# One attention block and one expert on one core: the same steps in another order, with about fifty of them on another engine

## The chip, the cores and the metric

The kernel runs on one core of one Trainium2 chip. The metric is the device time of one launch in microseconds. A profiled execution also gives a span, the time from the first to the last instruction of the core.

## The reference, cut to what matters

x has 2 batches of 2048 rows of 128 values. Two stages follow, each a layer norm, a network, a layer norm of its result and a sum.

```python
def attn(h, Wq, Wk, fc1_w, fc1_b, fc2_w, fc2_b):          # 1 head of 128
    q, k = rope(bf16(h @ Wq.T)), rope(bf16(h @ Wk.T))
    scores = (q @ k.T) / 128 ** 0.5
    o = where(causal, exp(scores), 0.0).sum(axis=-1)       # only the row sums are used
    return relu(o @ fc1_w.T + fc1_b) @ fc2_w.T + fc2_b     # 1 -> 16 -> 128

def ffn(x, W1, b1, W2, b2):                                # one of 16 experts has all the weight
    return relu(x @ W1[1] + b1[1]) @ W2[1] + b2[1]         # 128 -> 256 -> 128

x = x + layernorm(attn(layernorm(x)))
x = x + layernorm(ffn(layernorm(x)))
```

## The kernel before, in words

**Tiles.** The 4096 rows are 8 groups of 4 tiles of 128 rows; groups 0 to 3 are batch 0, groups 4 to 7 batch 1. Each stage has a list of the pieces it works on. FRONTS (norm, transpose, q, k and rope) are numbered 0 to 8: group 0 in two halves (0 and 1), then groups 1, 4, 5, 2, 6, 3, 7 as 2 to 8. BACKS (scores to the hidden layer) are groups 0, 1, 4, 5, 2, 6, 3 as 0 to 6, and the two halves of group 7 as 7 and 8. OUTS (the second product, last norm, sum and store) are the same as BACKS to 6 and then the four single tiles of group 7 as 7 to 10. Because of the causal mask a group needs the keys of the groups before it in its batch.

**Steps.** The whole program is the table STEPS, one word for each step, as `name.number`. A letter behind it gives the engine where there is a choice (A for ACT, D for DVE, P for POOL, which is GpSimd), and `#` gives the PSUM banks, of which there are eight. Each engine walks through the same table and issues, in that order, the steps that are its own. It waits on a semaphore for what a step reads, and where a bank was used before, until the user before has been emptied (Banks.free). So the table fixes the order on every engine, and an engine that waits holds up everything behind it in its own queue.

The steps of one piece are, in order:

- load_x (SP, DMA of x), stat1 (DVE, BN_STATS over pairs of tiles, L631), eps1 (variance plus epsilon, L354 on DVE and POOL, L602 on ACT), rstd1 (POOL, power of minus one half, L489), norm1 (x times rstd, L348);
- tr1 (PE, 4 transposes, L716), +tr1 (the copy out of PSUM, L505), q and k (PE, float32 matmuls, L724), +q and +k (copies to bfloat16, L505);
- the rotated half for rope either by swap (SP, two DMAs that exchange the partition halves, L336 and L337) or by rot (PE, L734); cos, sin (products with a table, L380 on POOL in two halves, L383 on DVE, L407 from PSUM) and rope (the sum, L414 to L417);
- scores.n.j.s (PE, L750 and the mask's L754) for row tile j and the key segment s: segment 0 is the keys of the first two groups of the batch, segment 1 those of the third and fourth, so that a group 2 or 3 of a batch can do its segment 1 before the first two are ready; exp (ACT, L553, in place, with the row sum); sum (DVE, L362 or L364), hT (PE, L761), +hT (ACT, relu, L522), fc2 (PE, L777 or L769);
- stat3, eps3, rstd3, x1 (the first stage's result, L664); stat4, eps4, rstd4, norm4, trz (PE, L716), +trz, h0 and h1 (PE, L724), +h0 and +h1 (relu with bias, ACT L528, DVE L530);
- y (PE, 8 matmuls of 128 columns for a group, L798, in some pieces on top of the bias by a matmul of ones, L788; in others bias on DVE, L679), stat5 (DVE L638 or ACT L609), eps5, rstd5, out (DVE L664, or ys on DVE, L650, and the sum on POOL, L496), store (SP, L341).

blank is a matmul on zeros whose result is not used (L693); blank.8 are eight of 512 columns. wqk and w1 centre the weights on PE, w2mean, b2mean and the like prepare the others on ACT. SP issues every DMA, in the order of the table. In the profile each float32 matmul stands as two instructions.

Of the kernel before, what the change touches and what calls it, by code (L numbers as in the profile page):

```python
# [35 lines left out]


STEPS = """
load_x.4 blank.8#7 blank.1.256#7 load_x.3 mask.0 load_wqk.0 load_x.1 load_x.0 repeat.0 stat1.4 load_fc.0 eps1.4.D
stat1.3 rstd1.4 load_x.6 wqk.0#0 load_x.8 eps1.3.A stat1.1 rstd1.3 eps1.1.A norm1.4.D load_x.5 blank.1#7 blank.1.256#7  # L40
+wqk.0.A load_x.2 stat1.0 tr1.4#1 rstd1.1 norm1.3.D load_b2.0 fc.0#0 +tr1.4.A load_table.1 norm1.1.P stat1.6 tr1.3#2
fcmean.0 load_table.0 q.4#1 eps1.0.D +tr1.3.A eps1.6.P stat1.8 load_x.7 rstd1.6 tr1.1#3 load_table.3 +q.4.A k.3#2
stat1.5 load_w2.0 +fc.0 rstd1.0 norm1.6.D q.3#1 load_table.2 eps1.8.D norm1.0.D tr1.6#4 +k.3.D rstd1.8 +q.3.A k.4#0
eps1.5.D +tr1.1.A stat1.2 swap.3 +tr1.6.A norm1.8.P tr1.0#3 stat1.7 +k.4.A q.1#1 load_table.4 k.6#4 cos.3.D w2mean.0
load_b1.0 eps1.2.D q.6#0 +tr1.0.D rstd1.2 +k.6.A swap.4 cos.4.D w2.0 q.0#3 sin.3.D +q.6.A tr1.8#4 load_w1.0 rstd1.5
k.0#2 b2mean.0 rope.3.D swap.6 +q.0.A k.1#0 +q.1.A norm1.2.D scores.2.3.0#3 +tr1.8.A scores.2.1.0#1 cos.6.D
scores.2.0.0#5 exp.2.3.0 scores.2.2.0#6 tr1.2#7 sin.4.D +k.1.A q.8#4 exp.2.1.0 cos.1.D exp.2.2.0 rope.4.D k.8#0 +k.0.A
+tr1.2.A eps1.7.D +q.8.D norm1.5.P scores.3.0.0#12 exp.2.0.0 +k.8.D scores.3.1.0#67 exp.3.0.0 rstd1.7 rot.1#5 sum.2.D
scores.3.3.0#34 swap.8 cos.8.D exp.3.1.0 hT.2#0 rot.0#1 sin.1.D cos.0.P k.2#2 exp.3.3.0 sin.0.D scores.3.2.0#56
rope.1.D +k.2.A q.2#7 rope.0.D +hT.2 sin.6.D exp.3.2.0 scores.0.1.0#2 scores.0.2.0#0 tr1.5#3 sin.8.D w1.0#4 +q.2.A  # L50
sum.3.D rope.8.D fc2.2#56 exp.0.1.0 swap.2 +tr1.5.A cos.2.D hT.3#7 scores.7.1.0#12 +w1.0.A rope.6.D scores.0.3.0#3
+hT.3 q.5#4 exp.7.1.0 stat3.2.D norm1.7.P k.5#7 +q.5.D exp.0.2.0 exp.0.3.0 eps3.2.D scores.5.3.0#12 sin.2.D exp.5.3.0
+k.5.D rstd3.2 scores.8.3.1#34 rope.2.D swap.5 exp.8.3.1 x1.2 cos.5.P scores.1.3.0#12 fc2.3#07 exp.1.3.0 stat4.2
scores.1.0.0#56 scores.0.0.0#3 tr1.7#4 stat3.3.D exp.1.0.0 scores.1.2.0#12 +tr1.7.D exp.0.0.0 eps3.3.P scores.1.1.0#56
exp.1.2.0 rstd3.3 sum.0.D sin.5.D q.7#4 exp.1.1.0 eps4.2.P x1.3 hT.0#1 scores.5.1.0#23 rstd4.2 +hT.0 scores.8.2.1#56
exp.5.1.0 rope.5.D fc2.0#01 +q.7.D norm4.2.P scores.4.2.1#7 exp.8.2.1 scores.4.1.1#2 stat3.0.D scores.4.0.1#3 k.7#4
exp.4.2.1 stat4.3 eps3.0.P scores.4.1.0#56 exp.4.0.1 rstd3.0 sum.1.D exp.4.1.1 +k.7.D trz.2#7 exp.4.1.0
scores.7.0.0#23 eps4.3.D +trz.2.D swap.7 rstd4.3 x1.0 exp.7.0.0 scores.5.0.0#45 norm4.3.P hT.1#6 h1.2#7 exp.5.0.0
stat4.0 scores.8.2.0#23 eps4.0.D +h1.2.D scores.4.2.0#01 +hT.1 rstd4.0 exp.8.2.0 scores.4.3.0#45 cos.7.D trz.3#7
sin.7.D h0.2#6 exp.4.3.0 +trz.3.D norm4.0.P scores.4.0.0#23 +h0.2.D exp.4.2.0 scores.4.3.1#7 trz.0#4 rope.7.D fc2.1#56  # L60
exp.4.3.1 +trz.0.D scores.6.0.0#01 exp.4.0.0 stat3.1.D h0.0#4 eps3.1.D exp.6.0.0 rstd3.1 scores.6.3.0#23 +h0.0.D
h0.3#7 exp.6.3.0 sum.4.D x1.1 hT.4#4 scores.6.2.1#01 +hT.4 scores.6.2.0#23 exp.6.2.1 stat4.1 scores.6.0.1#45 h1.0#6
+h0.3.D exp.6.0.1 fc2.4#01 exp.6.2.0 +h1.0.D scores.6.1.0#45 eps4.1.D stat3.4.D scores.6.3.1#67 rstd4.1 exp.6.1.0
y.2#2 eps3.4.D rstd3.4 norm4.1.D b2.0 exp.6.3.1 b2split.0 x1.4 scores.5.0.1#4 scores.5.2.1#5 exp.5.0.1 scores.5.1.1#3
scores.5.2.0#67 exp.5.2.1 bias.2.D scores.5.3.1#4 exp.5.1.1 scores.6.1.1#01 exp.5.2.0 trz.1#5 stat5.2.D h1.3#3
+trz.1.D eps5.2.P exp.6.1.1 rstd5.2 stat4.4 scores.8.3.0#67 y.0#5 exp.5.3.1 b2rows.0 eps4.4.P exp.8.3.0 rstd4.4
sum.5.D sum.6.D +h1.3.D hT.5#4 norm4.4.P scores.7.0.1#67 ys.2 +hT.5 scores.7.1.1#01 exp.7.0.1 bias.0.D hT.6#3 h0.1#4
out.2.P +hT.6 stat5.0.D exp.7.1.1 fc2.5#67 eps5.0.P store.2 h1.1#3 stat3.5.D sum.7.D fc2.6#01 +h0.1.D eps3.5.P +h1.1.A
rstd3.5 trz.4#2 stat3.6.A hT.7#3 y.1#4 rstd5.0 x1.5 eps3.6.A +trz.4.A rstd3.6 sum.8.D +hT.7 ys.0 h1.4#2 stat4.5
out.0.P h0.4#5 bias.1.D eps4.5.A +h1.4.A x1.6 fc2.7#3 rstd4.5 store.0 +h0.4.A hT.8#2 y.3#6 stat5.1.A stat4.6 norm4.5.P  # L70
stat3.7.D eps3.7.A eps4.6.D +hT.8 rstd4.6 trz.5#0 bias.3.D y.4#1 +trz.5.A stat5.3.D rstd3.7 norm4.6.D eps5.3.A x1.7
rstd5.3 fc2.8#0 trz.6#3 stat3.8.A out.3 h0.5#2 +trz.6.A eps3.8.A stat4.7 h1.5#5 store.3 rstd3.8 stat5.4.D eps4.7.A
+h0.5.A h0.6#6 rstd4.7 eps5.1.D x1.8 +h1.5.A rstd5.1 eps5.4.D h1.6#2 stat4.8 +h0.6.D y.5#5 rstd5.4 +h1.6.A norm4.7.D
eps4.8.D rstd4.8 ys.4 norm4.8.D trz.7#1 out.1 out.4.P stat5.5.A y.6#2 +trz.7.D eps5.5.A store.4 rstd5.5 store.1
trz.8#1 stat5.6.D h0.7#4 +trz.8.A h1.7#6 +h0.7.A eps5.6.P h0.8#1 +h1.7.D rstd5.6 h1.8#0 out.5 +h0.8.A y.7#6 +h1.8.A
y.8#1 stat5.7.A out.6 store.5 y.10#5 eps5.7.P stat5.8.A rstd5.7 y.9#0 stat5.10.A eps5.8.D store.6 out.7 rstd5.8
stat5.9.A eps5.10.D store.7 rstd5.10 eps5.9.A out.8 store.8 rstd5.9 out.10 store.10 out.9 store.9
# [761 lines left out]
```

## Time and profile before

| | |
|---|---|
| runs, us | 92.93, 95.62, 94.38 (median 94.38) |
| the profiled execution | 92.96 us |
| its span | 91.2 us |
| PE busy | 82.5 us (90%), 445 matmul instructions |
| DVE busy | 78.5 us (86%) |
| ACT busy | 70.7 us (78%) |
| POOL busy | 59.2 us (65%) |
| mean granted clock of TensorE | 0.992 |

The busy shares are over the whole span; PE's include time in which one matmul's end overlaps the next one's start. PE is the matmul part of TensorE, PEld its weight loads, DVE is VectorE, ACT is ScalarE, POOL is GpSimd and SP issues DMAs.

### The profile page before, as it was taken

The numbers are of one execution on the slowest core, as the hardware profiler recorded it, in microseconds if no ns is written. First come the engines' busy times: TensorE is split into PE (matmuls) and PEld (weight loads), VectorE is DVE, ScalarE is ACT, GpSimd is POOL, SyncE is SP. The second block draws the span as 40 slices with busy tenths as digits, with TensorE's granted clock in tenths as the row PEclk, the third lists the DMA queues.
The fourth block names the chain that finished last, engine by engine and source line by source line (L and its number), as shares of the span: only waits on it lengthen the run. The fifth ranks groups of instructions, "written<-read, shape, count | busy, mean of one in ns | idle before, by whom it ended". The sixth has DMA issues, their size and how long they took to land.

```text
span 91.2 us, 1530 instructions
## 1 busy us (share of the span) xinstructions
PE 82.5 (90%) x445; PEld 49.4 (54%) x445; DVE 78.5 (86%) x205; ACT 70.7 (78%) x201; POOL 59.2 (65%) x84
## 2 busy tenths in 40 slices
...
DMA packets 11884, 7.64 MB, mean 84 GB/s; under 512 B 851, under 2 KB 10980, under 8 KB 11876
## 3 DMA queue, kind: packets, MB, share of 16 engines
...
## 4 chain that ended last, share of the span: by engine, by line
PE 59%; ACT 14%; DVE 9%; DMA 7%; issue 3%; SPq 2%; POOL 2%; POOLq 1%; DVEq 0%
PE psum L724 19%; PE psum L798 14%; ACT psum L553 11%; PE psum L750 11%; PE psum L716 6%; DMA x_s<-x 4%; PE psum L777 3%; DMA qk_swap<-qk 3%; DVE rows_n L348 2%; POOL rstd L489 2%; ACT fc L566 2%; DVE qk_r L383 2%; DVE qk_swap L383 2%; PE psum L769 1%; DVE qk L505 1%
## 5 line engine op out<-in xcount | busy, mean ns | idle before, releaser
L489 POOL TENSOR_TENSOR rstd<-ve,half_neg 128x4 f32<-128x4 f32 (+2 forms) x38 | 35.0, 930 | 23.1 <-DVE ve L354 18.7
L553 ACT ACTIVATE psum<-psum 128x1024 f32<-128x1024 f32 (+7 forms) x48 | 36.6, 763 | 1.2 <-PE psum L754 0.8
L750 PE MATMUL psum<-qk_r 128*128 128x512 bf16 (+3 forms) x80 | 19.7, 348 | 1.7 <-DVE qk_r L417 1.0
L798 PE MATMUL psum<-w_c,hid 128*128 128x128 f32 x128 | 16.0, 277 | 0.0
L798 PEld LDWEIGHTS psum<-w_c,hid 128*128 128x128 f32 x128 | 15.5, 192 | 0.8 <-issue 0.3
L724 PE MATMUL psum<-cols_n,wqk 128*128 128x512 f32 (+1 forms) x36 | 15.8, 553 | 0.0
L724 PE MATMUL psum<-cols_n,w_c 128*128 128x512 f32 (+1 forms) x36 | 15.7, 550 | 0.0
L750 PEld LDWEIGHTS psum<-qk_r 128*128 128x128 bf16 x80 | 6.7, 98 | 13.0 <-ACT psum L553 4.8
L716 PE MATMUL psum<-ident,rows_n 128*128 128x128 f32 x64 | 10.2, 277 | 0.9 <-DVE rows_n L348 0.9
L638 DVE BATCH_NORM_STATS2 stats<-psum 128x6 f32<-128x256 f32 x23 | 8.7, 419 | 1.5 <-PE psum L798 1.0
L664 DVE SCALAR_TENSOR_TENSOR x<-psum,rstd,x_s 128x128 f32<-128x128 f32 x32 | 9.1, 343 | 1.0 <-POOL rstd L489 0.9
L716 PEld LDWEIGHTS psum<-ident,rows_n 128*128 128x128 f32 x64 | 7.3, 141 | 4.6 <-issue 2.1
L553 ACT ACTIVATION_READ_ACCUMULATOR psum<-psum 128x1 f32 x48 | 9.1, 189 | 0.0
L631 DVE BATCH_NORM_STATS2 stats<-x_s 128x6 f32<-128x256 f32 x16 | 6.2, 423 | 2.7 <-DMA x_s<-x 2.4
L505 ACT ACTIVATE cols_n<-psum 128x512 f32<-128x512 f32 (+1 forms) x11 | 6.0, 558 | 2.7 <-PE psum L716 2.7
L724 PEld LDWEIGHTS psum<-cols_n,w_c 128*128 128x128 f32 x36 | 6.1, 190 | 2.8 <-issue 2.0
L724 PEld LDWEIGHTS psum<-cols_n,wqk 128*128 128x128 f32 x36 | 6.1, 190 | 2.8 <-issue 1.4
L528 ACT ACTIVATE hid<-psum,b_s 128x512 f32<-128x512 f32 (+1 forms) x9 | 5.5, 615 | 2.7 <-PE psum L724 2.6
L609 ACT ACTIVATE rows_n<-psum 128x128 f32<-128x128 f32 x18 | 4.8, 278 | 3.2 <-PE psum L798 1.9
L602 ACT ACTIVATE ve<-stats,small 128x4 f32<-128x4 f32 (+2 forms) x10 | 3.0, 296 | 5.5 <-DVE stats L631 4.8
L530 DVE TENSOR_SCALAR hid<-psum,b_s 128x512 f32<-128x512 f32 (+1 forms) x9 | 6.4, 716 | 0.9 <-PE psum L724 0.7
L664 DVE SCALAR_TENSOR_TENSOR x_s<-psum,rstd,x 128x128 f32<-128x128 f32 x20 | 5.8, 345 | 1.1 <-POOL rstd L489 0.8
...
## 6 DMA issues: line engine op xcount, KB each, us to landing
...
```

What stands on the lines that cost most here:

```text
L489: ready[k].done(eng.tensor_tensor(rstd[:, g, STAT_SLOT[k], t], ve[:, g, STAT_SLOT[k], t], half_neg[:, 0:tiles], ALU.pow), n)
L505: return eng.activation(dst, src, ACT.Copy) if on_act else eng.tensor_copy(dst, src)
L528: ins = eng.activation(hid[:, g, h, c], src[:, 0:w], ACT.Relu, bias=b1_s[:, h:h + 1])
L530: ins = eng.tensor_scalar(hid[:, g, h, c], src[:, 0:w], b1_s[:, h:h + 1], 0.0, ALU.add, ALU.max)
L553: exps.done(eng.activation(area, area, ACT.Exp, scale=scale_qk, accum_out=sums[:, g, s, j:j + 1]), n, j, s)
L631: ins = eng.bn_stats(pair_stats(g, k, j), source[:, g, j:j + 2, :].rearrange("p t c -> p c t"))
L638: ins = eng.bn_stats(pair_stats(g, k, j0 + j), net_pair(k, n, j))
L664: ins = eng.scalar_tensor_tensor(dst[:, g, j0 + j, :], area, rstd[:, g, STAT_SLOT[k], j0 + j:j0 + j + 1], prev[:, g, j0 + j, :], ALU.mult, ...
L716: mm = eng.transpose(bank[:, j * P:(j + 1) * P], rows_n[:, g, j0 + j, :], ident[:, :])
L724: made[name].done(eng.matmul(bank_of(name, n)[:, 0:tiles * P], weight, cols_n[:, g, c], start=True, stop=True), n)
L750: mm = eng.matmul(psum[:, own[0] + i, 0:width], query, qk_r[:, g0 + c, 1, 0:width], start=True, stop=c < gb)
L798: mm = eng.matmul(bank[:, j * P:(j + 1) * P], hid[:, g, h, (j0 + j) * P:(j0 + j + 1) * P], w2_c[:, h, :], start=not seeded and h == 0, sto ...
```

## The change

Only the table of steps is another one. It holds the same 496 steps; the fillers blank.1.256 (twice) become blank.1.384 and blank.1.128. Its first words before and after:

```diff
-load_x.4 blank.8#7 blank.1.256#7 load_x.3 mask.0 load_wqk.0 load_x.1 load_x.0 repeat.0 stat1.4 load_fc.0 eps1.4.D
...
+load_x.1 blank.8#7 blank.1.384#7 load_x.3 mask.0 load_wqk.0 load_x.0 load_x.6 stat1.1 repeat.0 load_fc.0 eps1.1.A
...
```

What moves to another engine:

- to DVE: cos.5, norm1.1, norm1.8, norm4.0, norm4.5 (from POOL); +tr1.2, +tr1.4, +k.2, +h0.7, +w1, +wqk, stat3.6, stat5.1, stat5.5 (from ACT);
- to POOL: norm1.0, norm4.1, rope.8, sin.2 (from DVE);
- to ACT: +tr1.0, +k.3, +k.8, +q.8, +trz.1, +trz.7, +h0.0, +h0.6, stat5.0, stat5.3, stat5.4 (from DVE);
- of the 38 small eps steps, 20 change among the three.

The first load is x's piece 1 (128 KB) instead of piece 4 (256 KB). The line numbers of the changed file are one higher than those of the profile.

On DVE the first instructions now are the statistics of pieces 1 and 3, norm1.1, the statistics of piece 0, the weights' copy +wqk and norm1.3; then come the pairs of statistics of pieces 6, 4, 8 and 5 with norm1.6 among them, up to the rows below.

**DVE, the stretch around the first rope.** The names are stats (stat1), rows_n (norm1), ve (eps1), cols_n (+tr1), qk_r (cos, or rope where it reads itself) and qk_swap (sin). Before:

```order
L383 TENSOR_TENSOR qk_r<-qk,table 128x1024
L354 TENSOR_SCALAR ve<-stats 128x4
L505 COPY cols_n<-psum 128x256
L383 TENSOR_TENSOR qk_r<-qk,table 128x1024
L383 TENSOR_TENSOR qk_swap<-qk_swap,table 128x1024
L417 TENSOR_TENSOR qk_r<-qk_r,qk_swap 128x1024
L348 TENSOR_TENSOR rows_n<-x_s,rstd 128x512
L383 TENSOR_TENSOR qk_r<-qk,table 128x1024
```

Now:

```order
L349 TENSOR_TENSOR rows_n<-x_s,rstd 128x512
L632 BN_STATS stats<-x_s 128x6 x2
L384 TENSOR_TENSOR qk_r<-qk,table 128x1024
L349 TENSOR_TENSOR rows_n<-x_s,rstd 128x512
L506 COPY cols_n<-psum 128x512
L632 BN_STATS stats<-x_s 128x6 x2
L384 TENSOR_TENSOR qk_swap<-qk_swap,table 128x1024
L418 TENSOR_TENSOR qk_r<-qk_r,qk_swap 128x1024
L349 TENSOR_TENSOR rows_n<-x_s,rstd 128x512
```

The first rope is L417 before and L418 now, and norm1.2 stands behind it in both. Before, cos.4 and a copy of 256 columns stood ahead of the first sin; now it is norm1.4, norm1.8, two pairs of statistics and a copy of 512 columns, and cos.4 has gone behind.

**POOL, the first half.** rows_n is norm1 or norm4 (norm4 where it reads x1), qk_r is cos or rope, qk_swap is sin. Before:

```order
L489 TENSOR_TENSOR rstd<-ve,half_neg 128x4 x2
L348 TENSOR_TENSOR rows_n<-x_s,rstd 128x512
L489 TENSOR_TENSOR rstd<-ve,half_neg 128x4
L380 TENSOR_TENSOR qk_r<-qk,table 128x256 x2
L348 TENSOR_TENSOR rows_n<-x_s,rstd 128x512
L489 TENSOR_TENSOR rstd<-ve,half_neg 128x4
L380 TENSOR_TENSOR qk_r<-qk,table 128x512 x2
L354 TENSOR_SCALAR ve<-stats 128x4
L489 TENSOR_TENSOR rstd<-ve,half_neg 128x4
L354 TENSOR_SCALAR ve<-stats 128x4
L489 TENSOR_TENSOR rstd<-ve,half_neg 128x4
```

Now:

```order
L355 TENSOR_SCALAR ve<-stats 128x4
L490 TENSOR_TENSOR rstd<-ve,half_neg 128x4
L349 TENSOR_TENSOR rows_n<-x_s,rstd 128x512
L490 TENSOR_TENSOR rstd<-ve,half_neg 128x4 x2
L349 TENSOR_TENSOR rows_n<-x_s,rstd 128x512
L381 TENSOR_TENSOR qk_r<-qk,table 128x256 x2
L381 TENSOR_TENSOR qk_swap<-qk_swap,table 128x512 x2
L355 TENSOR_SCALAR ve<-stats 128x4
L490 TENSOR_TENSOR rstd<-ve,half_neg 128x4
L416 TENSOR_TENSOR qk_r<-qk_r,qk_swap 128x512 x2
L490 TENSOR_TENSOR rstd<-ve,half_neg 128x4 x2
```

Two halves of sin.2 and two of rope.8 have come, and the two halves of cos.5 have gone; rstd and eps of the first stage's results stand behind them.

**PE, around the last scores.** 128x512 x2 at L750 is one score step over two banks. Before:

```order
L750 MATMUL psum<-qk_r 128x512
L750 MATMUL psum<-qk_r 128x256
L754 MATMUL psum<-later,ident_b 128x128
L761 MATMUL psum<-ident,osum 128x128
L724 MATMUL psum<-cols_n,w1_c 128x512
L777 MATMUL psum<-fc2,h1T 128x256 x2
L724 MATMUL psum<-cols_n,w1_c 128x512
L777 MATMUL psum<-fc2,h1T 128x256 x2
L716 MATMUL psum<-ident,rows_n 128x128 x4
L761 MATMUL psum<-ident,osum 64x128
L798 MATMUL psum<-w2_c,hid 128x128 x8
```

Now:

```order
L751 MATMUL psum<-qk_r 128x256
L755 MATMUL psum<-later,ident_b 128x128
L799 MATMUL psum<-w2_c,hid 128x128 x8
L751 MATMUL psum<-qk_r 128x512 x2
L762 MATMUL psum<-ident,osum 128x128
L799 MATMUL psum<-w2_c,hid 128x128 x8
L717 MATMUL psum<-ident,rows_n 128x128 x8
L778 MATMUL psum<-fc2,h1T 128x256 x2
L725 MATMUL psum<-cols_n,w1_c 128x512
L762 MATMUL psum<-ident,osum 64x128
L725 MATMUL psum<-cols_n,w1_c 128x512 x3
L770 MATMUL psum<-fc2,h1T 128x256
```

Before, the last scores (512 and 256 columns and the mask's L754) are followed by hT, h0, fc2, h1, fc2; now one y (L799, eight of them) stands ahead of the last scores (512 columns twice, scores.8.3.0) and one behind, then two trz, and one fc2 of 512 columns and one of 256 (L770) are left behind them.

## Rows read from the trace of the kernel before

**Rows 1.** The page's chain that ended last, shares of the span by engine.

```profile
PE 59%; ACT 14%; DVE 9%; DMA 7%; issue 3%; SPq 2%; POOL 2%; POOLq 1%; DVEq 0%
```

**Rows 2.** Windows of the whole core; busy us of each engine, granted clock.

```profile
core 0: us, PE busy (x) PEld busy (x) DVE busy (x) ACT busy (x) POOL busy (x), PEclk, DMA share, GB/s
17.00:24.00 7.00, 6.24 (x31) 2.94 (x30) 7.00 (x12) 6.09 (x19) 4.15 (x5) 1.00 0.38 95
42.00:52.00 10.00, 10.00 (x47) 4.65 (x45) 9.48 (x24) 10.00 (x23) 4.30 (x4) 1.00 0.08 19
64.00:76.00 12.00, 12.00 (x79) 8.95 (x78) 10.06 (x30) 7.97 (x32) 9.23 (x10) 1.00 0.16 46
```

**Rows 3.** Timeline of PE, head: start, us, engine, line, operation, tiles, [idle before].

```profile
5.64 0.67 PE L699 MATMUL psum<-wqk_f,center 128*128 128x256 f32 x2 [0.88 <-DMA wqk_f<-wqk_t]
...
17.15 0.38 PE L750 MATMUL psum<-qk_r 128*128 128x512 bf16 x1
```

**Rows 4.** Timeline of DVE, head.

```profile
3.50 0.76 DVE L631 BATCH_NORM_STATS2 stats<-x_s 128x6 f32<-128x256 f32 x2 [1.63 <-DMA x_s<-x]
...
5.92 0.43 DVE L631 BATCH_NORM_STATS2 stats<-x_s 128x6 f32<-128x256 f32 x1 [0.80 <-DMA x_s<-x]
...
15.52 0.69 DVE L383 TENSOR_TENSOR qk_swap<-qk_swap,table 128x1024 bf16<-128x1024 bf16 x1 [0.24 <-DMA qk_swap<-qk]
...
16.92 1.53 DVE L348 TENSOR_TENSOR rows_n<-x_s,rstd 128x512 f32<-128x512 f32 x1
...
22.40 1.17 DVE L383 TENSOR_TENSOR qk_r<-qk,table 128x1024 bf16<-128x1024 bf16 x1
```

**Rows 5.** Timeline of ACT: first exponential, a full one, its four waits, the last.

```profile
17.62 0.58 ACT L553 ACTIVATE psum<-psum 128x512 f32<-128x512 f32 x1
...
21.26 0.69 ACT L553 ACTIVATE psum<-psum 128x640 f32<-128x640 f32 x1 [0.76 <-PE psum L754]
...
22.77 1.01 ACT L553 ACTIVATE psum<-psum 128x1024 f32<-128x1024 f32 x1
...
27.94 0.46 ACT L522 ACTIVATE h1T<-psum,fc 128x128 f32<-128x128 f32 x1 [0.40 <-PE psum L761]
...
30.85 1.01 ACT L553 ACTIVATE psum<-psum 128x1024 f32<-128x1024 f32 x1 [0.27 <-PE psum L750]
...
61.15 0.46 ACT L522 ACTIVATE h1T<-psum,fc 128x128 f32<-128x128 f32 x1 [0.37 <-PE psum L761]
...
62.56 0.80 ACT L553 ACTIVATE psum<-psum 128x768 f32<-128x768 f32 x1
```

**Rows 6.** Timeline of PE, from the last scores to the last tile of y.

```profile
61.66 0.28 PE L761 MATMUL psum<-ident,osum 128*128 128x128 f32 x1
...
62.73 0.70 PE L777 MATMUL psum<-fc,h1T 64*128 64x256 f32 x4
...
71.80 0.60 PE L716 MATMUL psum<-ident,rows_n 128*128 128x128 f32 x4
...
86.78 0.66 PE L798 MATMUL psum<-w_c,hid 128*128 128x128 f32 x4
```

**Rows 7.** Timeline of POOL (GpSimd), head.

```profile
12.26 1.04 POOL L348 TENSOR_TENSOR rows_n<-x_s,rstd 128x512 f32<-128x512 f32 x1
14.29 1.98 POOL L489 TENSOR_TENSOR rstd<-ve,half_neg 128x4 f32<-128x4 f32 x2 [0.99 <-DVE ve L354]
16.36 1.55 POOL L348 TENSOR_TENSOR rows_n<-x_s,rstd 128x512 f32<-128x512 f32 x1
...
21.73 1.30 POOL L380 TENSOR_TENSOR qk_r<-qk,table 128x256 bf16<-128x256 bf16 x2
```

**Rows 8.** Groups by line and form, ACT's copies of q and k.

```profile
L505 ACT ACTIVATE qk<-psum 128x512 bf16<-128x512 f32 x7 | 4.2, 595 | 0.5 <-PE psum L724 0.3
```

**Rows 9.** The page's group of the score matmuls: busy us, mean ns, idle before.

```profile
L750 PE MATMUL psum<-qk_r 128*128 128x512 bf16 (+3 forms) x80 | 19.7, 348 | 1.7 <-DVE qk_r L417 1.0
```

**Rows 10.** Chain that ended last, in order of time: the first swap's second half.

```profile
13.01 2.49 DMA qk_swap<-qk
```

More of the change, by code:

```diff
@@ L44 @@
[L44 to L73, printed above, removed]
```

49 lines of the change are left out of this document (40 added, 9 removed).

## Prediction

> **What bounds the kernel now.** I read the page first: of the span of 91.2 us the chain that ended last lies 59% on PE and 14% on ACT [rows 1]. That is a mean over stages, so the windows come next [rows 2]. From 17 to 24 us it is DVE that is full (7.00 of 7.00) while PE and ACT have gaps; from 42 to 52 ACT and PE are both full; from 64 to 76 PE is full (12.00 of 12.00) and ACT is not (7.97). So there are three limits in a row: the head, bound by the loads and DVE; the stretch of the exponentials, bound by ACT with PE close behind; and the end, bound by PE. The granted clock is 1.00 of its upper level in all of them.
>
> The head is read in the timelines of PE and DVE [rows 3, 4]. The first tile group's statistics start at 3.50 us, when x_s has landed; the matmul on Wq and Wk waits for its DMA until 5.64; the first scores start at 17.15. ACT [rows 5] starts its first exponential at 17.62 and ends its last at 62.56 + 0.80 = 63.36: 45.74 us, of which 1.80 are waits (0.76, 0.40, 0.27 and 0.37, in brackets there). From 61.66, when the last scores are through, PE runs to its last tile of y at 86.78 with nothing to wait for [rows 6], and 4.42 us of span lie behind that start.
>
> **The change part by part.** The same operations are done in both: 48 exponentials, the same matmuls and transposes, the same DMAs and bytes. Only the order, the banks and the engine of about 50 steps change. The two fillers of blank columns trade 512 columns for 512 others; they stand in time in which PE waits for loads, and cost nothing while it does. I take the three limits in turn.
>
> *Head.* The first load is now one of 128 KB, then 256, then the weights: these end 512 KB down the queue, and x.0 ends 640 KB down it. Before, 256 KB had landed at 3.50 and 768 KB at 5.92 [rows 4], that is 212 KB/us. So the weights come at 3.50 + 256/212 = 4.7 instead of 5.64, and x.0 at 5.3. PE then has tr1.1 and, after the copy of the weights on DVE, its first q at about 6.2. From there DVE's own queue decides when the first scores can start, because rope.3 stands 18 steps behind x.0's statistics on it. From x.0's landing: its statistics 0.4, the weights' copy 0.35, four norms at 0.60 (a product's 0.69 less the overlap with the next), six pairs of statistics at 0.76, three eps at 0.1, and cos.3, the copy of tr1.4, sin.3 and rope.3 at 0.60 each [rows 4]. That is 0.4 + 0.35 + 2.4 + 4.6 + 0.3 + 2.4 = 10.4, so rope.3 ends at 15.7; with 0.3 for the wait for rstd1.3 and for landings, 16.0. The same three pairs of q and k and the two short ones are in front of the first scores on PE in both orders. Scores start at 16.0 instead of 17.15, and since a transpose stands between the first two, the first exponential starts 1.0 behind: 17.0 instead of 17.62.
>
> Against it stands what DVE and GpSimd do to each other. The norm of 16.92 took 1.53 us instead of about 0.69. It began inside GpSimd's product of 16.36, which ended at 17.91, and ended itself 0.54 later; the product of 22.40 took 1.17 and ended 0.54 behind GpSimd's two halves, at 23.03 [rows 4, 7]. So a DVE product of two operands in SBUF stood still until GpSimd's was done. The Trainium skill (SBUF — State Buffer, Who interferes with whom) says this as a rule: such an instruction and one of GpSimd that reads SBUF take a shared pair of ports in turn, and whoever starts first keeps it for the whole instruction. The trace agrees for products. It does not for rstd: the product that ran from 15.52 to 16.21 took no more than 0.69 beside the two powers of 14.29 to 16.27 [rows 7], so I count no clash with a power. In the changed order norm1.5 on GpSimd (1.04) comes by my count at 12.3 to 13.3, just where norm1.8 stands on DVE. If it starts first, DVE loses up to 0.9 and the first scores start at 16.9, the first exponential at 17.9, 0.3 later than before. The clash may also not occur. I take the middle: first exponential at 17.4, 0.2 earlier.
>
> *Exponentials.* ACT's other work between first and last exponential changes from two short copies, four long ones and the W1 copy (2 x 0.38 + 4 x 0.60 + 0.39 = 3.6) to four long copies, b2mean 0.5, +h0.0 0.69 and an eps of 0.30 (3.9), the long ones by [rows 8]: +0.3. The wait of 0.76 was for scores that wait for rope.4; now scores.5.2.1 and 5.3.1 (group 6 against its own keys alone) stand ahead and fill it. I keep the other 1.0 us of waits, as nothing here says that they go. ACT thus ends exp.6.1.1, the last but one, at 63.36 - 0.2 + 0.3 - 0.76 less the last one's 1.01 [rows 5] = 61.7.
>
> *End.* scores.8.3.0 takes the banks that exp.6.1.1 frees, so PE stands there until then: 61.7 + 0.5 = 62.2 for hT.6 behind it, against 61.66. Behind it PE has less than before: fc2 of two groups (0.63 each, its 0.70 less the overlap) and an hT (0.1) are gone to the front, and one trz (0.44) has come; one y left and one came. That is 0.93 less than 86.78 - 61.66 = 25.12, so 24.19. The last y starts at 62.2 + 24.2 = 86.4 instead of 86.78. The 4.42 behind it stay: the four single tiles, their rstd on GpSimd and the four stores stand in the same order. Sum: 0.4 us by this path with half a clash, 0.8 without it.
>
> The cover of this sum is ACT's 1.0 us of waits. Each that the new order also fills counts in full, since PE's own path (first scores at 16.0, then at most the 69.6 us from 17.15 to 86.78, in which the scores alone waited 1.7 [rows 9]) would reach the last y at about 84. The bounds are therefore: all waits gone and no clash, first exponential 17.0: 86.4 - 0.4 - 1.0 = 85.0, a gain of 1.8; a full clash and 0.76 not won: 86.4 + 0.5 + 0.76 = 87.7, a loss of 0.9. Between ends so far apart I take -0.6, nearer to the sum than to either. The profiled execution took 92.96 us, so the forecast is 92.4. Those 92.96 stand at the lowest of the three runs shown (92.93; median 94.38, highest 95.62), so a median of runs may lie up to 1.4 above such a figure; the range has that inside. 2% is 1.9 us, about what a measurement of this kernel can tell from no change.
>
> **The rivals.** First, *the fill works fully*: no clash in the head, ACT without waits between 17.0 and 61, DVE in front of PE at the end. For it: DVE has about 1 us less in all (products moved to GpSimd, copies to ACT), and ACT's queue has more exponentials that need only one group. Against it: PE and ACT are full in 42 to 52 already. The gain is 1.8 to 2.5, 90.8 us.
>
> Second, *the gain is taken back*: ACT gets about 2 us of work more in all (copies and squares), the clash occurs and other DVE products meet one of GpSimd's six half products of cos, sin and rope, where it had four (1.30 for two of 256 columns [rows 7], so about 1.25 for one of 512). What is won in the head is waited for in the middle: 92.9, between 92.6 and 93.9.
>
> Third, and slower: *rope.8 on GpSimd starves ACT*. Group 7's rope comes at the end of a new chain through both engines. +k.2 ends on DVE 12 instructions behind rope.3, at 16.0 + 6 = 22; its swap lands 3.1 later (0.5 for the first issue, 2.5 and 0.1 behind the second [rows 10]), at 25.1; then sin.2 on GpSimd 2.5, eps and rstd 1.2, x1.2 on DVE 1.1, cos.8 0.6, rope.8 on GpSimd 2.5, with some 0.3 of passing on: 33.3, and 34.2 with the clash. ACT needs scores.7.0.0 after 22 exponentials of 13,440 columns in all (0.84 ns a column and 0.15 us each, from the 0.58 of 512 and the 1.01 of 1024 columns [rows 5]: 14.6) and 3.1 of copies, at 17.0 + 17.7 = 34.7. The slack is 0.5 to 1.4. As soon as two more clashes of 0.9 fall on DVE's or GpSimd's part of it, ACT and PE stand, and everything behind x1.2 with them. At three clashes and the queues behind them the price is 2 to 3: 92.96 + 2.2 = 95.2.
>
> The Trainium skill's rule (SBUF — State Buffer, Who interferes with whom) would, if it held for the powers too, put rstd1.8 and rstd1.5 in DVE's way as well and lead to this third case, 95.2; the product beside the powers in [rows 7] speaks against that, and its chance is inside the 0.15.
>
> **How the numbers follow.** The forecast, a gain of 0 to 1.5, gets 0.42; the full fill 0.24; the gain taken back 0.19; the starved ACT 0.15. The likeliest time is 92.4, its own range 91.4 to 93.0. For 8 in 10 the range reaches from 90.8, the first rival, to 95.0, the third, with the run-to-run spread inside. Faster by over 2% needs 91.1 or less: the full fill and a little of the forecast, 0.25. Slower by over 2%: the third rival and a little of the second, 0.16. Within 2%: 0.59.
>
> **What would show it.** Right: wqk's matmul before 5.0, the first scores between 15.9 and 17.0, no ACT wait of 0.7 near 21, DVE without idle time until 24, the wait of PE at scores.8.3.0 put down to ACT, the last y 24.2 us behind it. A DVE norm of some 1.5 us near 12.5 shows the clash. Wrong: PE's last scores well before ACT is done with them (then PE, not ACT, was the limit), a wait of PE for GpSimd's rope.8 before scores.7.0.0, or ACT waiting for DVE's results in the middle.

## The result and the profile after

| | before | changed |
|---|---|---|
| first comparison, median of its runs | 95.0 us (4 runs, 92.93 to 95.95) | 93.97 us (4 runs, 93.87 to 94.15) |
| first comparison, ratio | | 1.0105 [1.0063, 1.0147] |
| second comparison, median of its runs | 93.86 us (29 runs) | 93.62 us (12 runs) |
| second comparison, ratio | | 1.0031 [0.9987, 1.0076] |
| profiled execution | 92.96 us, span 91.2 | 94.05 us, span 92.2 |

Over all runs of the study 45 of the 97 executions that begin with the order of the kernel before lie over 1.5% above the fastest of their kernel, against 3 of the 100 that begin with the changed order, and the ratios leave all these out (of the first comparison's four of the kernel before only 92.93 remains), which is why they and the plain medians point in opposite directions. By the ratios the change makes the kernel 1.0% slower in the first comparison and 0.3% in the second, whose interval has 1 in it; in the mean that is about 0.6 us. I had forecast 92.4 us, 0.6 us faster.

The page's chain, which answers to [rows 1], has gone over from PE and DVE to ACT (14% before):

```profile
PE 53%; ACT 34%; POOL 4%; DVE 4%; issue 1%; POOLq 1%; DVEq 0%
```

The windows that answer to [rows 2]:

```profile
core 0: us, PE busy (x) PEld busy (x) DVE busy (x) ACT busy (x) POOL busy (x), PEclk, DMA share, GB/s
17.00:24.00 7.00, 7.00 (x36) 3.74 (x34) 6.21 (x13) 7.00 (x24) 2.42 (x2) 1.00 0.59 142
...
32.00:42.00 10.00, 9.18 (x50) 4.32 (x48) 9.87 (x28) 10.00 (x27) 6.73 (x7) 1.00 0.18 40
42.00:52.00 10.00, 9.28 (x45) 4.33 (x45) 9.27 (x27) 10.00 (x24) 5.69 (x6) 1.00 0.01 2
```

From 17 to 24 us DVE is no longer full (6.21 instead of 7.00); PE and ACT are, both with 7.00. The fill that I had expected took place. But ACT is full from there on and PE is not.

The timeline of PE, against [rows 3] and [rows 6]: the centring of Wq and Wk, the first q, the first scores, its waits in the middle, the last scores and the last tile of y.

```profile
5.07 1.19 PE L700 MATMUL psum<-wqk_f,center 128*128 128x256 f32 x2
...
7.16 1.13 PE L725 MATMUL psum<-cols_n,wqk 128*128 128x256 f32 x4
...
17.29 0.27 PE L751 MATMUL psum<-qk_r 128*128 128x256 bf16 x1
...
29.01 0.50 PE L751 MATMUL psum<-qk_r 128*128 128x512 bf16 x2 [0.75 <-DVE qk L506]
37.62 0.45 PE L751 MATMUL psum<-qk_r 128*128 128x512 bf16 x2 [0.55 <-ACT psum L554]
40.63 1.04 PE L751 MATMUL psum<-qk_r 128*128 128x512 bf16 x4 [0.22 <-ACT psum L554]
42.75 0.59 PE L751 MATMUL psum<-qk_r 128*128 128x512 bf16 x2 [0.64 <-ACT psum L554]
...
61.33 2.00 PE L799 MATMUL psum<-w_c,hid 128*128 128x128 f32 x16
63.17 0.59 PE L751 MATMUL psum<-qk_r 128*128 128x512 bf16 x2
63.60 0.27 PE L762 MATMUL psum<-ident,osum 128*128 128x128 f32 x1
...
87.83 0.66 PE L799 MATMUL psum<-w_c,hid 128*128 128x128 f32 x4
```

The first q comes 1.6 us earlier than before (8.77 there), and yet the first scores come 0.14 later than in [rows 3]: PE does the same transposes, products of q and k and products for fc in front of the first scores in both orders, and before, more of them stood ahead of the first q. The wait for DVE's copy at 29.01 is new. The timeline of ACT, against [rows 5]:

```profile
9.77 0.38 ACT L506 ACTIVATE cols_n<-psum 128x256 f32<-128x256 f32 x1 [0.41 <-PE psum L717]
...
18.40 0.61 ACT L554 ACTIVATE psum<-psum 128x512 f32<-128x512 f32 x1
...
29.60 0.80 ACT L554 ACTIVATE psum<-psum 128x768 f32<-128x768 f32 x1 [0.83 <-PE psum L755]
58.31 0.46 ACT L523 ACTIVATE h1T<-psum,fc 128x128 f32<-128x128 f32 x1 [0.34 <-PE psum L762]
...
61.62 0.80 ACT L554 ACTIVATE psum<-psum 128x768 f32<-128x768 f32 x1
63.80 1.01 ACT L554 ACTIVATE psum<-psum 128x1024 f32<-128x1024 f32 x1 [1.26 <-PE psum L751]
```

Between the copy at 9.77 and the wait at 29.60 the timeline of ACT has no wait. Its first exponential starts at 18.40 instead of 17.62, behind 8.63 us of its own queue. The wait of 0.76 near 21 is gone, as forecast; one of 0.83 has come at 29.60. What lies behind that one is in DVE's timeline, and beside it in that of GpSimd:

```profile
26.37 0.69 DVE L384 TENSOR_TENSOR qk_r<-qk,table 128x1024 bf16<-128x1024 bf16 x1
26.97 1.38 DVE L418 TENSOR_TENSOR qk_r<-qk_r,qk_swap 128x512 bf16<-128x512 bf16 x1
28.27 0.68 DVE L506 CAST qk<-psum 128x512 bf16<-128x512 f32 x1
```

```profile
26.92 2.44 POOL L381 TENSOR_TENSOR qk_swap<-qk_swap,table 128x512 bf16<-128x512 bf16 x2 [1.52 <-DMA qk_swap<-qk]
```

rope.1 (L418, 512 columns) took 1.38 us; the rope of this size before it, at 25.43, took 0.43. GpSimd had started the first of its two halves of sin.2 at 26.92, 0.05 before rope.1. The half ended at about 28.14 and rope.1 at 28.35. +k.5 stands right behind rope.1 on DVE, PE's scores wait for +k.5, and ACT waits for those scores.

To see which stretch the time comes from, I cut each profile of the study at four instants: the first exponential; PE's last wait for ACT (0.64 in the changed kernel, 0.51 before); the last tile of y; the end of the span.

| kernel | first q | first exponential | PE's last wait for ACT | from one to the other | last y | from that wait |
|---|---|---|---|---|---|---|
| before | 8.77 | 17.62 | 41.47 | 23.85 | 86.78 | 45.31 |
| before, again | 8.71 | 17.87 | 41.97 | 24.10 | 87.28 | 45.31 |
| changed | 7.16 | 18.40 | 42.75 | 24.35 | 87.83 | 45.08 |
| changed, again | 6.87 | 18.07 | 42.39 | 24.32 | 87.45 | 45.06 |

From the means, the changed kernel has its first exponential 0.49 later (18.24 against 17.75), loses 0.36 up to PE's last wait, and wins 0.24 behind it: 0.61 us at the last y, the 0.7% of the two ratios' mean. The 0.49 rests on two profiles of each. Four of the kernels below have the changed head unaltered, and over all six profiles of it (table at the end of the experiments) the first exponential is at 18.04 in the mean, 17.76 to 18.40: 0.29 behind the kernel before, with the quickest of the six ahead of the slower of its two. So a loss in the head is likely but not shown clear of the scatter; the one in the middle is (24.35 and 24.32 against 23.85 and 24.10). There are two causes to be tested, the head and the middle.

### The profile page after: what moved, and what is told of

Its sections match the earlier page's. It is cut to its first block, busy times and chain, and to the rows that moved or that the text cites. A ratio compares the mean times of both kernels' runs of the same rounds, so it can differ in the third digit from the quotient of the medians.

```text
span 92.2 us, 1537 instructions
## 1 busy us (share of the span) xinstructions
PE 84.8 (92%) x445; PEld 49.7 (54%) x445; DVE 78.7 (85%) x204; ACT 71.7 (78%) x205; POOL 59.2 (64%) x82
## 4 chain that ended last, share of the span: by engine, by line
PE 53%; ACT 34%; POOL 4%; DVE 4%; issue 1%; POOLq 1%; DVEq 0%
ACT psum L554 20%; PE psum L725 16%; PE psum L799 14%; PE psum L751 7%; ACT qk L506 6%; PE psum L717 5%; PE psum L694 4%; ACT cols_n L506 3%; PE psum L778 2%; POOL rstd L490 2%; DVE qk_r L418 1%; ACT fc L567 1%; POOL qk_r L381 1%; PE psum L770 1%; PE psum L700 1%
## 5 line engine op out<-in xcount | busy, mean ns | idle before, releaser
L490 POOL TENSOR_TENSOR rstd<-ve,half_neg 128x4 f32<-128x4 f32 (+2 forms) x38 | 36.0, 953 | 19.2 <-DVE ve L355 15.5
L751 PE MATMUL psum<-qk_r 128*128 128x512 bf16 (+3 forms) x80 | 21.0, 349 | 2.5 <-ACT psum L554 1.4
L799 PE MATMUL psum<-w_c,hid 128*128 128x128 f32 x128 | 16.2, 278 | 0.0
L799 PEld LDWEIGHTS psum<-w_c,hid 128*128 128x128 f32 x128 | 15.4, 192 | 0.9 <-issue 0.7
L717 PE MATMUL psum<-ident,rows_n 128*128 128x128 f32 x64 | 10.3, 281 | 0.0
L603 ACT ACTIVATE ve<-stats,small 128x4 f32<-128x4 f32 (+2 forms) x12 | 3.6, 296 | 4.6 <-DVE stats L632 3.1
L529 ACT ACTIVATE hid<-psum,b_s 128x512 f32<-128x512 f32 (+1 forms) x10 | 6.3, 644 | 1.1 <-PE psum L725 1.1
L755 PE MATMUL psum<-later,ident_b 128*128 128x128 bf16 x32 | 6.7, 219 | 0.0
L506 ACT ACTIVATE qk<-psum 128x512 bf16<-128x512 f32 (+1 forms) x13 | 6.4, 531 | 0.0
```

Source lines behind the costliest of these rows:

```text
L490: ready[k].done(eng.tensor_tensor(rstd[:, g, STAT_SLOT[k], t], ve[:, g, STAT_SLOT[k], t], half_neg[:, 0:tiles], ALU.pow), n)
L506: return eng.activation(dst, src, ACT.Copy) if on_act else eng.tensor_copy(dst, src)
L529: ins = eng.activation(hid[:, g, h, c], src[:, 0:w], ACT.Relu, bias=b1_s[:, h:h + 1])
L717: mm = eng.transpose(bank[:, j * P:(j + 1) * P], rows_n[:, g, j0 + j, :], ident[:, :])
L751: mm = eng.matmul(psum[:, own[0] + i, 0:width], query, qk_r[:, g0 + c, 1, 0:width], start=True, stop=c < gb)
L755: mm = eng.matmul(psum[:, own[0] + i, width - P:width], ident_b[:, 0:P], later[:, :], start=False, stop=True)
```

## The experiments

Four runs asked which stretch makes the loss, four more asked about single mechanisms, and the last four repeated and built on the answer.

**e_rope1: rope.1 behind the copy of k.5.** Nothing else changes; rope.1 is not needed until later.

```diff
-exp.3.2.0 rope.0.D ... cos.2.D q.5#7 rope.1.D exp.0.0.0 fc2.2#03 exp.5.3.0 sin.2.P +k.5.D
+exp.3.2.0 rope.0.D ... cos.2.D q.5#7 exp.0.0.0 fc2.2#03 exp.5.3.0 sin.2.P +k.5.D rope.1.D
```

> The changed kernel with one step moved: rope.1 on DVE stands behind +k.5 instead of ahead of it. Clash theory (rope.1 stood still beside sin.2 on GpSimd, 1.38 us instead of 0.43, and +k.5, PE and ACT waited behind it): +k.5 starts near 27.0 instead of 28.27, PE's wait of 0.75 and ACT's of 0.83 are gone, the span falls by 0.7 to 0.8 to about 91.4. Head theory (what counts is that ACT's first exponential starts at 18.4 instead of 17.6, and ACT is full from there): the wait goes, but another of about the same size comes before 47 us, span 92.0 to 92.3.

Measured: 92.55 us (92.2 to 92.77), ratio 0.9978 [0.9941, 1.0015]. DVE's timeline of this run:

```profile
25.83 0.69 DVE L384 TENSOR_TENSOR qk_r<-qk,table 128x1024 bf16<-128x1024 bf16 x1
26.43 0.68 DVE L506 CAST qk<-psum 128x512 bf16<-128x512 f32 x1
27.04 0.78 DVE L418 TENSOR_TENSOR qk_r<-qk_r,qk_swap 128x512 bf16<-128x512 bf16 x1
```

The copy now follows the product of 25.83 at once. rope.1 again ends 0.2 behind GpSimd's first half (26.37 to about 27.60), but nobody waits for it. PE's wait falls to 0.20 at 29.13, and ACT has no wait at all from 17.86 to 56.87. From the first exponential to PE's last wait for ACT it is 17.86 to 41.30, 23.44 instead of 24.35. Behind it there are 45.08, as in the changed kernel. The head theory, which wanted another wait of the same size before 47 us, falls; the clash theory's span (91.4) was 0.6 above the measured one (90.8). So the clash is worth 0.9 us here. The other 0.5 by which this profile is ahead lies in front of the first scores (16.75 against 17.29), where the order is the same: that is a difference between executions, and it needed repeats.

**h_headbefore: the order of the kernel before up to its first scores, the changed one behind them.**

> The kernel before up to its first scores, then the changed order for all that is left. Head theory: first exponential at 17.6, span 0.8 below the changed kernel's 92.2, so 91.4. Clash theory: the head does not matter, since the wait for +k.5 near 28 is still there, 92.0 to 92.3.

Measured: ratio 1.0112 [1.006, 1.0164], from three of the six runs (93.68 to 93.88 us, spans of 91.9 to 92.1). Joining the two does not win back what the changed order loses. The spans are about those of the clash theory, but the only trace, of an execution of 96.7 us, has no clash in it: rope.1 started at 30.44, 0.16 ahead of GpSimd's half, and took 0.42. So the number decides for neither theory.

**h_headafter: the changed order up to its first scores, that of before behind them.**

> The changed order up to its first scores, then the order of the kernel before. Head theory: the first exponential near 18.4 and the span 0.8 above the 91.2 of the kernel before, 92.0. Clash theory: no clash with sin.2 in this order, span 91.2 or, since ACT has waits to fill, a little less.

Measured: 95.68 us, ratio 1.0296 [1.0248, 1.0345], a span of 94.0 where the theories had 92.0 and 91.2. Its timeline of PE and two of its windows show why:

```profile
22.71 0.43 PE L751 MATMUL psum<-qk_r 128*128 128x512 bf16 x2 [2.06 <-DVE qk_r L418]
...
35.01 0.59 PE L751 MATMUL psum<-qk_r 128*128 128x512 bf16 x2 [0.96 <-DVE qk_r L418]
```

```profile
17.00:24.00 7.00, 4.65 (x25) 2.30 (x24) 4.37 (x9) 4.57 (x17) 1.28 (x2) 0.95 0.44 110
24.00:32.00 8.00, 8.00 (x34) 4.12 (x33) 7.31 (x14) 6.77 (x16) 2.44 (x3) 0.83 0.31 69
```

The head prepares other groups than those that the second half asks for first, so PE waits 2.06 for a rope at 22.71, and ACT behind it 2.43 at 23.23. PE is busy in 4.65 of 7.00 there, and in the next 8 us its granted clock is 0.83 on average, so part of them ran at the lower level, 1.2 GHz. Both hybrids measure the joint and not a half. They don't decide between head and middle; an order of this kind is cut in two only at that price.

**e_w2late: less work for ACT in the head.** w2mean, w2 and b2mean, 1.8 us of ACT, stand in front of b2 near 48 us and no longer between 15 and 20.

```diff
-... tr1.8#0 w2mean.0 rstd1.2 q.4#1 sin.3.D +q.6.A w2.0 k.4#4 ... +tr1.2.D b2mean.0 load_w1.0
+... tr1.8#0 rstd1.2 q.4#1 sin.3.D +q.6.A k.4#4 ... +tr1.2.D load_w1.0
...
-... stat3.7.D b2.0 rstd4.1
+... stat3.7.D w2mean.0 w2.0 b2mean.0 b2.0 rstd4.1
```

> The changed kernel with w2mean, w2 and b2mean (1.75 us of ACT in the head) moved to just before b2 near 48 us. Head theory: the first exponential starts near 17.1, ACT is through with the work that PE waits for 1.3 to 1.75 us earlier, and the span falls to about 91. If PE takes over as the limit sooner, only PE's waits between 30 and 47 (about 1.5) can go, 90.9 to 91.4. Clash theory: no change, 92.2.

Measured: 94.13 us, ratio 1.0137 [1.009, 1.0184], a span of 92.4 where the theories had about 91 and 92.2. The first exponential comes at 18.09 and not near 17.1, now with waits of ACT for PE in front of it (0.73 at 16.36, 0.16 at 18.09). In the two profiles of the changed order whose first q is also at 6.87 it comes at 18.06 and 18.07: take ACT's 1.8 us away, and PE's queue is as long.

From the first exponential to PE's last wait for ACT (41.57) it is 23.48, 0.9 less than in the changed kernel. The moved work is not what won that, for e_rope1 has 23.44 without moving it. The clash did not occur here, though the order around rope.1 is that of the changed kernel:

```profile
26.51 0.42 DVE L418 TENSOR_TENSOR qk_r<-qk_r,qk_swap 128x512 bf16<-128x512 bf16 x1
26.84 0.69 DVE L506 CAST qk<-psum 128x512 bf16<-128x512 f32 x1
```

```profile
26.63 2.42 POOL L381 TENSOR_TENSOR qk_swap<-qk_swap,table 128x512 bf16<-128x512 bf16 x2 [1.76 <-DMA qk_swap<-qk]
```

This time rope.1 started 0.12 ahead of GpSimd's half, took 0.42, and the copy followed at once. What PE is ahead at 41.57 it loses behind it: from there to the last y (87.96) it is 46.39 instead of 45.08, with waits of 0.70 and 0.26 for ACT at 54.08 and 55.00. Work of ACT is not free near 48 us: 1.8 us of it cost 1.3 there.

**after_again: the changed kernel itself.**

> The changed kernel itself once more, unchanged, to see how much of it is the execution and how much the order. Theory (the clash at rope.1 makes the loss in the middle): rope.1 again takes 1.2 to 1.4 us beside sin.2's first half on GpSimd, +k.5 starts about 1.9 us behind the start of cos.2's product, PE waits 0.6 to 0.9 for it, and the ratio is 1.008 to 1.014. Rival (the head makes the loss, and only its rate differs between executions of the same order): the first matmul on Wq and Wk takes 0.6 in some executions and 1.2 in others, and where it takes 0.6 the whole kernel is 0.4 to 0.6 us shorter; then the times of this kernel scatter over 0.5 us or more.

Measured: 93.62 us, ratio 1.0031 [0.9987, 1.0076], below the 1.008 to 1.014 of the theory; one of the twelve executions took 471 us and is left out. rope.1 took 1.38 again (26.64), PE waited 0.75 again for the copy behind it (28.67), and the middle is 24.32. The clash is in both traces of the changed kernel and in that of e_y0 (rope.1 at 26.33, 1.38), and absent in the one of e_w2late. What differs from the first profile is the head: 18.07 for the first exponential instead of 18.40.

**e_sin2: sin.2 on VectorE**, in place of GpSimd's two halves.

```diff
-exp.5.3.0 sin.2.P +k.5.D
+exp.5.3.0 sin.2.D +k.5.D
```

> As the changed kernel, but the sin.2 product is done by VectorE (one instruction of 1024 columns, 0.69) and no longer by GpSimd's two halves. Theory (rope.1 stands still because GpSimd's half of sin.2 holds the access to SBUF): rope.1 takes 0.43 instead of 1.38; VectorE has the 0.6 of sin.2 more, but only when its swap has landed at about 26.9, so +k.5 starts at 28.0 to 28.1 instead of 28.27, PE's wait there is 0.4 to 0.6 instead of 0.75, and the time is 93.5 to 94.0. Rival (rope.1 is slow for a reason of its own, for example its inputs coming late): rope.1 stays at 1.2 to 1.4, sin.2 comes on top, +k.5 starts at 28.8, and the time is 94.3 to 94.8.

Measured: 93.28 us (93.09 to 93.44), ratio 0.9996 [0.9959, 1.0032].

```profile
26.05 0.69 DVE L384 TENSOR_TENSOR qk_r<-qk,table 128x1024 bf16<-128x1024 bf16 x1
26.65 0.42 DVE L418 TENSOR_TENSOR qk_r<-qk_r,qk_swap 128x512 bf16<-128x512 bf16 x1
26.99 0.69 DVE L384 TENSOR_TENSOR qk_swap<-qk_swap,table 128x1024 bf16<-128x1024 bf16 x1
27.59 0.68 DVE L506 CAST qk<-psum 128x512 bf16<-128x512 f32 x1
```

With GpSimd out of the way, rope.1 in the same place takes 0.42. The rival (rope.1 is slow by itself) falls. From the first exponential (18.08) to PE's last wait for ACT (42.04) it is 23.96, 0.4 less than in the changed kernel, and not the whole 0.9 less, as sin.2 now stands on DVE in front of the copy. The copy starts 1.54 behind the product of 26.05 instead of 1.90, and PE's wait is 0.39 instead of 0.75. This is the direct test: the 0.95 that rope.1 took more comes from GpSimd's product. The time was 0.2 under the range I had given; I had worked it out from the first profile's head (18.40), and here the first exponential was at 18.08.

**e_y0: y.0 behind scores.8.3.0 on PE.**

```diff
-... eps4.4.D stat3.5.D y.0#1 exp.6.1.1 b2rows.0 eps3.5.D rstd3.5 sum.6.D scores.8.3.0#56 rstd4.4
+... eps4.4.D stat3.5.D exp.6.1.1 b2rows.0 eps3.5.D rstd3.5 sum.6.D scores.8.3.0#56 y.0#1 rstd4.4
```

> As the changed kernel, but y.0 stands behind scores.8.3.0 on PE instead of in front of it. Theory (the end is PE's: from scores.8.3.0 on it is full, and ACT's wait of 1.26 before its last exponential costs nothing): scores.8.3.0 starts about 1.7 us sooner and waits up to 0.5 for exp.6.1.1's bank, ACT's wait of 1.26 shrinks below 0.5, and the last y and the time stay within 0.3 of the changed kernel's (93.7 to 94.2). Rival (the last exponential's lateness is what the end waits for, through sum.8 and norm4): the time falls by 0.8 to 1.3, to 92.8 to 93.1.

Measured: 94.73 us, ratio 1.0147 [1.0079, 1.0214]. Both expectations are wrong. PE's timeline:

```profile
60.60 0.22 PE L755 MATMUL psum<-later,ident_b 128*128 128x128 bf16 x1
62.14 0.38 PE L751 MATMUL psum<-qk_r 128*128 128x512 bf16 x1 [1.32 <-ACT psum L554]
```

PE comes to scores.8.3.0 at about 60.8 and stands 1.32 for the banks that exp.6.1.1 frees, and the last y starts at 88.28, 46.20 behind PE's wait of 42.08 instead of 45.06 to 45.08. In the changed kernel y.0's 1.84 us (61.33 to 63.17) fill just that wait: y.0 is the cover.

**r1_w2late: e_rope1 and e_w2late together.**

> The changed kernel with rope.1 behind +k.5 (92.55 in its run) and w2mean, w2 and b2mean (1.8 us of ACT) moved from the head and the start of the exponentials to the place before b2.0. Theory (between 28 and 42 us ACT is the bound, PE waited 1.4 us for it there; after 42 PE is): the waits at 36 to 41 go, PE reaches 45 us about 1 us earlier, and what ACT has more around 48 us costs PE 0.3 to 0.8 again: 91.9 to 92.3. Rival (ACT is the bound until its last exponential, so that its work counts wherever it stands): the last exponential is where it was, within 0.2, and so is the time, 92.4 to 92.8.

Measured: 94.1 us, ratio 1.009 [1.0049, 1.0131]: 1.3% above the mean of the two runs of e_rope1's kernel (0.9978 and 0.9948). Both theories miss. The waits for ACT near 55 are the known ones (0.68 and 0.26), and three for DVE come on top between 30 and 33 (0.16, 0.20, 0.38): the second swap of group 2 was issued in 1.25 us instead of 0.60 in e_rope1 and its rows came at 27.67 instead of 26.37. Why the issue took longer stays open.

**before_again: the kernel before itself.**

> The kernel before once more, unchanged, for a second profile of its head and middle. Theory: its head is set by the wait for Wq and Wk's DMA, so the first scores come again within 0.3 of 17.15, the first exponential within 0.3 of 17.62, and from PE's last wait for ACT (41.47) to the last y it is again 45.3. Rival (its head scatters by as much as that of the changed kernel, so that the two heads don't differ but by chance): the first exponential comes 0.4 or more away from 17.62.

Measured: 93.35 us, ratio 0.999 [0.9954, 1.0025]. The first scores at 17.40, the first exponential at 17.87, 45.31 at the end. Its head scatters by 0.25. That is less than the 0.49 between the two kernels' means of two profiles, and about the 0.29 that is left with all six profiles of the changed head.

**r1_again: e_rope1 once more.**

> The changed kernel with rope.1 behind +k.5 once more (0.998 of before in its first run), beside the two that build on it. Theory (the clash at rope.1 cost 0.9 us in the middle): first exponential to PE's last wait for ACT is 23.4 again, where the changed kernel had 24.3; ratio 0.993 to 1.002. Rival (the first run was quick by its head alone): ratio 1.003 or more.

Measured: 92.69 us (92.43 to 93.07), ratio 0.9948 [0.9921, 0.9975]. From the first exponential (18.06) to PE's last wait for ACT (41.62) it is 23.56, though this head was as slow as that of the changed kernel's repeat. So the clash costs 0.8 to 0.9 in the middle, and without it the changed order is 0.3 to 0.7 quicker there than the kernel before (23.85 and 24.10), where PE waits 0.97 and 1.22 for a rope (at 32.27 and 32.76) and the changed order has no such wait. This order beats the changed kernel in both comparisons and the one before by 0.2% and 0.5%, the second time by more than its interval.

**r1_wqk: and the weights' copy in front of the statistics of x.0 on VectorE.**

```diff
-eps1.3.A load_table.0 rstd1.3 stat1.0 tr1.1#1 load_x.5 +wqk.0.D
+eps1.3.A load_table.0 rstd1.3 +wqk.0.D stat1.0 tr1.1#1 load_x.5
```

> As the kernel before this one, and the copy of the centred Wq and Wk on VectorE moved in front of the statistics of x.0, behind which it waits for x.0's DMA. Theory (the whole head hangs on the first q, 10.1 us of PE's work in front of the first scores and 8.6 of ACT's in front of the first exponential): the first q comes at 6.2 to 6.3 instead of 6.64 where PE runs at its full rate by then, so the first scores come at 16.3 to 16.4, the first exponential at 17.4 to 17.5, and the ratio falls by 0.003 to 0.004. Rival (VectorE's queue sets the head, as I predicted): x.0's statistics slip by the copy's 0.35, rope.3 with them, and the first exponential and the time stay the same or get 0.2 later.

Measured: 92.69 us, ratio 0.9954 [0.9926, 0.9982], the same as r1_again. The profiled execution had the Wq and Wk matmul at the slower rate, so that the copy waited for it, and not for x.0:

```profile
4.87 1.06 PE L700 MATMUL psum<-wqk_f,center 128*128 128x256 f32 x2
5.72 0.64 PE L717 MATMUL psum<-ident,rows_n 128*128 128x128 f32 x2
6.15 0.61 PE L694 MATMUL psum<-blank 128*128 128x512 bf16 x2
6.83 1.13 PE L725 MATMUL psum<-cols_n,wqk 128*128 128x256 f32 x4
```

The first q could not come at 6.2 then. Neither theory's numbers are met in full (the rival's "the same" is, but its reason, x.0's statistics slipping, is not: rope.3 is at 15.89 as in r1_again).

**r1_head: and without the second group of blank matmuls.** Left out are 512 and 128 columns of a product that nobody reads.

> As r1_wqk, and without the second group of blank matmuls (512 and 128 columns) in front of the first q. Theory (they stand in time in which PE waits anyway when it runs at full rate, and cost up to 0.3 when it runs at half): the first q is at 6.2 to 6.4 in any execution, and the time is that of r1_wqk or up to 0.2 less, with less scatter. Rival (they keep PE's rate up): without them the matmuls between 6 and 10 us run at half rate, the head takes 1 us or more longer, and the ratio is above 1.005.

Measured: 92.64 us, ratio 0.9945 [0.9916, 0.9973]. The first q is at 6.84 and not at 6.2 to 6.4, with the matmuls behind it as quick as with the blanks. So the second group of blanks neither costs nor helps anything that can be measured.

Six profiles of the changed head with the copy in its place give the dependence that I had left out of my sum:

| kernel | Wq, Wk matmul (2 parts) | first q | first scores | behind the first q | first exponential |
|---|---|---|---|---|---|
| e_y0 | 4.83, 0.60 | 6.56 | 16.65 | 10.09 | 17.76 |
| e_rope1 | 4.70, 0.60 | 6.64 | 16.75 | 10.11 | 17.86 |
| e_sin2 | 5.01, 0.67 | 6.72 | 16.98 | 10.26 | 18.08 |
| r1_again | 4.88, 0.87 | 6.87 | 16.96 | 10.09 | 18.06 |
| changed, again | 4.88, 1.06 | 6.87 | 16.96 | 10.09 | 18.07 |
| changed | 5.07, 1.19 | 7.16 | 17.29 | 10.13 | 18.40 |

Whatever the first q does, the first scores are 10.1 to 10.3 us behind it and the first exponential 1.1 behind those. From 8 to 16 us PE is full in both profiles of the changed kernel.

## Why the prediction was wrong, step by step

**Head, the first q (said: weights at 4.7, x.0 at 5.3, first q at about 6.2).** The weights came at 4.7 to 5.1, as computed. x.0 came between 5.66 (e_y0) and 5.97 (r1_again): the term was 0.4 to 0.7 too small, because I had taken the queue's mean of 212 KB/us from two landings of another order. The copy of the weights stands behind x.0's statistics on DVE and so waited for it too (0.55 at the first q in e_rope1). And PE's matmul on the weights, now at the very start, took 1.06 or 1.19 in some executions and 0.60 in others; I had 0.67 from [rows 3], where it stood 0.6 later. The first q came at 6.56 to 7.16. As the first scores follow it at a fixed distance, this is what made the first exponential later than my 17.4.

**Head, what follows (said: DVE's own queue decides, 10.4 behind x.0, first scores at 16.0, first exponential 1.0 behind).** The 10.4 were right: 5.96 to 16.58 is 10.6 in the repeat of the changed kernel. But DVE was not the limit: its first rope was through at 16.58 there and the first scores came at 16.96. This is the step that failed in the head. PE has 10.1 us of work between its first q and the first scores (in the kernel before it had 17.15 - 8.77 = 8.38), and ACT 8.6 between its copy of tr1.0 and the first exponential. I summed neither queue. With them the first exponential would have been put at 6.2 + 10.1 + 1.1 = 17.4 even with my too early q. That is the middle value I used for another reason (half a clash in the head), so there the two errors cancelled by luck. With the true first q it is 17.8 to 18.4. e_w2late shows that both queues are about equally long: without ACT's 1.8 us it gained nothing.

**Clash in the head (said: up to 0.9 if norm1.5 and norm1.8 meet).** They met, and GpSimd lost: norm1.8 on DVE started at 13.42 and took 0.69, norm1.5 at 13.47 and took 1.54 instead of 1.04. DVE lost nothing, so the 0.4 that I had put in for it was not there.

**Exponentials (said: ACT's other work +0.3, the wait of 0.76 gone, 1.0 of waits stay).** From the first exponential to the end of exp.6.1.1 I had 17.4 to 61.7, 44.3. Measured: 18.40 to 62.42, 44.0. The size was right, the contents were not, and that is luck: of the waits that I had kept only 0.34 at hT was left, and the clash put 0.83 in the place of the others. The sum left this clash out, and that is the step which turned the sign. The second rival had said that other products of DVE would meet GpSimd's six half products, and named 1.25 as the length of each; that is where the forecast went. The rival that starved ACT by rope.8 did not come about. rope.8's halves ran at 33.51 and no scores waited for them.

The clash itself is the rule of the Trainium skill (SBUF — State Buffer, Who interferes with whom) with this case's numbers: of a DVE product of two operands in SBUF and a GpSimd product the one that starts first keeps the access. At rope.1 GpSimd was first by 0.05 us, and rope.1 ended 0.2 behind the half, a little sooner than the 0.42 that it takes alone would have it. In e_w2late rope.1 was first by 0.12, and took its 0.42. I had used the rule for the head alone and not gone along the rows of GpSimd's other halves. The order did show sin.2 on GpSimd and a rope on DVE with a copy behind it that PE needs.

**End (said: PE stands at scores.8.3.0 until exp.6.1.1 is done, hT.6 0.5 behind it, then 24.19 to the last y, then 4.42).** hT.6 came 1.18 behind exp.6.1.1 and not 0.5, as PE was still on y.0. I had not laid y.0's 1.84 against the wait. The 24.19 measured 24.23 (63.60 to 87.83), the 4.42 measured 4.37. e_y0 shows that PE would stand there without y.0.

**The sum.** Against the first profile: first exponential 1.0 later than 17.4; 0.3 less to the end of exp.6.1.1; 0.7 more to hT.6; the rest as computed: 86.4 + 1.0 - 0.3 + 0.7 = 87.8, and 87.83 was measured. Between the forecast (-0.6) and the mean result (+0.6) lie 1.2 us, and the clash is 0.8 to 0.9 of them. With rope.1 moved, the same order has its last y at 86.38 and 86.67, where the sum had 86.4, and is 0.2 to 0.5% faster than before. That agreement is luck too: in these two profiles the first exponential is 0.5 and 0.7 later than 17.4, the way from there to the end of exp.6.1.1 is 43.12 and 43.21 instead of 44.3, and hT.6 comes 0.7 later. Of the 1.1 to 1.2 in the middle 0.7 are waits of ACT that I had kept; the rest is not explained.

**The statement that held the sum together** was "PE's own path would reach the last y at about 84", by which I took ACT's waits for free cover. It counted PE's work from first scores at 16.0, which PE's own queue did not allow.

What stays open: why the matmuls around 5 us take twice as long in some executions as in others (not for the second group of blanks, which stands behind them); how often the clash occurs over many executions, as three traces of the unaltered stretch have it and two have not; how much the changed head loses by itself; and why one swap's issue took 1.25 us in r1_w2late.
